# Selecting three batches early and running three experts while the last batch is selected

## What is computed

```python
logits = jnp.einsum('bsd,de->bse', x, Wg) + bg
probs = jax.nn.softmax(logits, axis=-2)          # over the tokens of a batch
vals, idx = jax.lax.top_k(jnp.transpose(probs, (0, 2, 1)), 128)
tok = x[bidx, idx]                               # 128 tokens per batch and expert
h = relu(einsum('bekd,edo->beko', tok, w1) + b1)
h = relu(einsum('bekd,edo->beko', h, w2) + b2)
h = einsum('bekd,edo->beko', h, w3) + b3
out = zeros.at[bidx, idx].add(h * vals)
```

## Time and profile before

| | us |
|---|---|
| median of 3 runs | 4139.88 (4139.71 to 4147.63) |
| profiled execution, its time | 4138.08 |
| its span, first to last instruction | 4136.3 |
| PE busy in the span | 3837.9 (93%) |
| DVE, ACT, POOL busy | 2483.1, 1566.9, 904.0 |
| granted clock, mean | 0.978 of full |

### The profile page before, as it was taken

How to read it: one execution, slowest core, us unless ns; L and a number is a source line. 1 busy time by engine, 2 the same in 40 slices (tenths; PEclk the granted TensorE clock), 3 DMA queues, 4 the chain that set the end, 5 groups by cost and what they waited for, 6 DMA issues and landing times. The chain is left out here.

```text
span 4136.3 us, 91192 instructions
## 1 busy us (share of the span) xinstructions
PE 3837.9 (93%) x36924; PEld 2346.8 (57%) x36924; DVE 2483.1 (60%) x4839; ACT 1566.9 (38%) x3178; POOL 904.0 (22%) x1017
## 2 busy tenths in 40 slices
PE   5999999999999999999999999999999948999996
PEld 2677645656776456567754565677545623444445
DVE  3777535877775368777744587777446872222224
ACT  2444225854442258544422584444135720000002
POOL 2333200223331012233310022333101202222221
PEclk8999999999999999999999999999999979999998
DMA  8333449744333487443335873433358725666676
GB/s 259 105 92 97 126 169 316 269 130 112 96 95 116 188 310 266 127 116 95 95 104 203 305 265 119 116 96 96 103 221 297 265 86 127 157 147 157 148 181 189
DMA packets 323147, 678.60 MB, mean 164 GB/s; under 512 B 28432, under 2 KB 125760, under 8 KB 319504
## 3 DMA queue, kind: packets, MB, share of 16 engines
q1 hardware_dynamic: 275152, 621.65, 46.9%
q0 software_dynamic: 15024, 34.41, 4.5%
q10 hardware_dynamic: 32576, 16.92, 1.9%
HBM read 388.31 MB, written 210.11 MB: 145 GB/s over the span
## 5 line engine op out<-in xcount | busy, mean ns | idle before, releaser
L530 ACT ACTIVATE sc<-sc,nmax 128x1024 f32<-128x1024 f32 x516 | 591.7, 1147 | 777.0 <-DVE nmax L756 776.4
L487 POOL TENSOR_SCALAR sc<-sc,pinv 128x1024 f32<-128x1024 f32 x516 | 576.5, 1118 | 1198.8 <-DVE pinv L764 1185.6
L1088 PE MATMUL psum<-pts,wct 32*64 32x256 f32 x8192 | 460.2, 376 | 9.0 <-PEq L1083 4.6
L1088 PE MATMUL psum<-xall,wct 32*64 32x256 f32 x8192 | 458.9, 376 | 6.1 <-issue 6.0
L1073 PE MATMUL psum<-xt,w_all 128*128 128x256 f32 x1792 | 415.7, 385 | 23.6 <-PEq L1070 23.6
L886 DVE CUSTOM_DVE_ANT_0 sc<-psum,big 128x896 f32<-128x896 f32 (+7 forms) x512 | 364.0, 753 | 102.9 <-PE psum L1294 87.2
L781 DVE STREAM_TRANSPOSE pts<-sc 128x1024 f32<-128x1024 f32 (+3 forms) x342 | 333.6, 976 | 130.6 <-PE psum L1088 87.0
L1073 PEld LDWEIGHTS psum<-xt,w_all 128*128 128x128 f32 x1792 | 332.5, 190 | 128.3 <-issue 67.0
L530 ACT ACTIVATE sc<-sc,xmax 128x896 f32<-128x896 f32 (+7 forms) x512 | 394.8, 773 | 11.7 <-DVE xmax L886 11.6
L756 DVE CUSTOM_DVE_ANT_0 sc<-psum,table_a 128x1024 f32<-128x1024 f32 x258 | 312.1, 1210 | 110.0 <-PE psum L1031 92.5
L1088 PEld LDWEIGHTS psum<-pts,wct 32*64 32x64 f32 x8192 | 310.6, 132 | 99.8 <-issue 54.8
(11 more groups left out here) (194 smaller groups left out, 5362.0 us busy)
## 6 DMA issues: line engine op xcount, KB each, us to landing
wct<-xall SPq DMA_DIRECT2D x576, 128.0 KB, 2.4
big<-skew_d SPq DMA_DIRECT2D x48, 1024.0 KB, 5.4
w_sb<-w_dram SPq DMA_DIRECT2D x45, 1024.0 KB, 5.7
big<-skew_d SPq DMA_DIRECT2D x48, 768.0 KB, 4.4
big<-skew_d SPq DMA_DIRECT2D x32, 896.0 KB, 5.3
big<-skew_d SPq DMA_DIRECT2D x32, 640.0 KB, 7.0
w_all<-wqkv_dram SPq DMA_DIRECT2D x33, 512.0 KB, 3.5
skew_d<-pts SPq DMA_DIRECT2D x8, 2048.0 KB, 6.6
```

The lines of the kernel that those rows point to most:

```text
L487: pool.tensor_scalar(sc[k % 4][:, :], sc[k % 4][:, :], pinv[:, k % 4:k % 4 + 1], 1.0, ALU.mult, ALU.mult).then_inc(probs_scaled, 1)
L530: act.activation(tile, tile, ACT.Exp, bias=least, scale=-1.0, accum_out=total).then_inc(probs_ready, 1)
L1088: mm = pe.matmul(OSUM[HEAD[h], a, :], v_all[rows, ST * (b % GROUPS) + b // GROUPS, HEAD[h]], ptf[h][rows, QG * b:QG * b + QG], start=(b == ...
```

## The change

Batches 0 to 2 stay in block 1's loop, batch 3 is written out behind it (`batch(B - 1, last=True)`). In the written-out batch:

- The selection of batches 0 to 2 (96 rows) runs on DVE inside self-attention. SP loads their logits during pair 0 (`load_held`), the maximum and the scaling stand at the first pair border, rounds 0 to 6 at the ends of pairs 1 to 7, rounds 7 to 15 between the row tiles of the output projection. PE turns and flips the lists there, DVE merges behind the first copied block, and PE waits for `picks_done` before the first relative product. The scratch tiles are parts of `xr` and `pts`, so `x` of batch 3 is loaded in two halves, the second after round 8.
- POOL gathers expert 0's tokens of batches 0 to 2 at unit 24 of cross-attention. SP loads expert 0's `w1` and `w2` at unit 26, in the place of the next batch's `xT`, weights and tables.
- The prefetch for a next batch is left out. PE transposes expert 0's tokens, then the normalized rows, then come the logits. SP copies them straight from SBUF to SBUF with eight DMAs.

In block 2, six steps stand ahead of the loop: experts 0, 1, 2 over batches 0 to 2, then the same experts over batch 3. Batch 3's selection (32 rows) runs on DVE under the first of them; ACT takes its exponentials behind step 0's second layer, PE turns its lists inside step 2's first layer. Tokens of these steps are transposed by PE and copied by ACT. Ahead of the loop, which now runs experts 3 to 13, the tokens of expert 3 and of expert 15 are gathered, turned and spread, the spreads on SP's queue ahead of the loop's loads.

```diff
+FIRST_EXPERTS = (0, 1, 2)
+F = len(FIRST_EXPERTS)
 LAST_EXPERTS = (E - 2, E - 1)
+SOONER, LATER = (0, 1, 2), (3,)
 FINISH = ((0, 1), (2,), (3,))
-STEPS = [(e, group) for group in FINISH for e in LAST_EXPERTS]
+STEPS = [(e, group) for group in (SOONER, LATER) for e in FIRST_EXPERTS] + \
+        [(e, group) for group in FINISH for e in LAST_EXPERTS]
 TAKEN = [sum(len(group) for _, group in STEPS[:s]) for s in range(len(STEPS) + 1)]
+BEHIND = 2 * F
+PICKS = TOPK // 8
+SOONER_ROWS, LATER_ROWS = E * len(SOONER), E * len(LATER)
 EXTRA = 2
 WXN = 3 * DC * P + EXTRA
...
+        def selection(dve, done, i, groups, pr, held, row_no, lists, above, best):
+
+            count, (lo, hi) = E * len(groups), (groups[0], groups[-1] + 1)
...
+            def scale_rows():
+
+                dve.wait_ge(row_exp_ready, 2 * i + 2)
+                done(dve.tensor_tensor(rinv[0:n, :], rsum[0:n, 0:1], rsum[0:n, 1:2], ALU.add))
+                done(dve.reciprocal(rinv[0:n, :], rinv[0:n, :]))
+                done(dve.tensor_scalar(held[0][0:n, :], held[0][0:n, :], rinv[0:n, 0:1], None, ALU.mult))
+
+            def pick(r):
+
+                now = held[r][0:n, :]
+                eight = top[0:n, 8 * r:8 * r + 8]
+                done(dve.max(eight, now))
+                ins = dve.max_index(top_at[0:n, 8 * r:8 * r + 8], eight, now)
+                if r < PICKS - 1:
+                    ins = dve.match_replace(held[r + 1][0:n, :], eight, now, -1.0)
+                done(ins)
+
+            def number_rows():
+
...
+                def load_held():
+
+                    sp.wait_ge(x2_stored, 32)
+                    sp.sem_inc(x2_stored, -32)
+                    sp.wait_ge(logits_stored, 16 * GROUPS)
+                    sp.dma_start(held_flip, flip_in).then_inc(flip_loaded, 16)
+                    flat = logit_d.rearrange("b e n -> (b e) n")
+                    for i in range(2):
+                        for j in range(2):
+                            sp.dma_start(held_pr[SOONER_ROWS * i:SOONER_ROWS * i + SOONER_ROWS, j, :],
+                                         flat[0:SOONER_ROWS, HALF * (i ^ j):HALF * (i ^ j) + HALF]
+                                         ).then_inc(held_loaded, 16)
 
                 def next_wqk(hp):
...
+                    sp.wait_ge(held_moved, 1)
+                    sp.dma_start(xr[:, ST // 2:ST, :], x[b, HALF:S, :].rearrange("(t p) d -> p t d", p=P)
+                                 ).then_inc(xr_loaded, 16)
...
+                        if u == PRELOAD[0]:
+                            for free in (w_free, *table_free):
+                                sp.wait_ge(free, 1)
+                            for n, w in enumerate((w1, w2)):
+                                sp.dma_start(w_front[n], w[0].rearrange("(c p) n -> p c n", p=P)).then_inc(we_loaded[n], 16)
+                        continue
...
+                                sp.dma_start(last_pr[E * i:E * i + E, j, QG * k:QG * k + QG],
+                                             last_lg[DH * g:DH * g + E, :]).then_inc(lg_loaded, 16)
+                    return
...
+                    if last and u == NU // 2:
+                        pool.wait_ge(picks_done, 1)
+                        pool.wait_ge(xt_free, 1)
+                        for b in SOONER:
+                            pool.indirect_dma_start(tok[:, b, :], None, x2_d[0:S * len(SOONER), :],
+                                                    bass.IndirectOffsetOnAxis(ap=rows[:, b, 0:1], axis=0)
+                                                    ).then_inc(step_gathered[b], 16)
...
+                    copy_first_tokens(act, 0, tokT)
+                    root_of_variance()
+                    even_transposes(x2t)
+                    return
...
+                    dve.memset(top[:, :], 0.0)
+                    dve.wait_ge(held_loaded, 64)
+                    row_max()
+                    cross_border(scale_rows)
                     add_biases()
+                    pick(0)
+                    for hp in range(2, PAIRS):
+                        cross_border()
+                        add_biases()
+                        pick(hp - 1)
...
+                    if last and t < 5:
+                        for r in range((7, 9, 11, 13, 14)[t], (9, 11, 13, 14, 16)[t]):
+                            pick(r)
+                        if t == 0:
+                            dve.sem_inc(held_moved, 1)
+                        if t == 4:
+                            number_rows()
+                    if last and t == ST - 2:
+                        copy_lists((BANK[6][:, 0:P], BANK[7][:, 0:P]))
...
+                    odd_transposes(x2t)
+                    dve.wait_ge(logits_ready, 1)
+                    done(dve.tensor_scalar(last_lg, LOGITS, bg_sb[:, 0:1], None, ALU.add))
+                    dve.sem_inc(logits_out, 1)
+                    return
...
+                    if last and t == ST - 1:
+                        turn_picks(pe, 0, held_row_no, (BANK[6][:, 0:P], BANK[7][:, 0:P]))
...
+                    first_tokens(pe, 0)
+                    transpose_rows()
...
+            sp.dma_start(w_e[2], w3[0].rearrange("(c p) n -> p c n", p=P)).then_inc(we_loaded[2], 16)
+            sp.dma_start(flip[:, :], flip_in).then_inc(flip_loaded, 16)
+            for j in range(F - 1):
+                for n, w in enumerate((w1, w2, w3)):
+                    sp.dma_start(first_w[j + 1][n], w[FIRST_EXPERTS[j + 1]].rearrange("(c p) n -> p c n", p=P)
+                                 ).then_inc(next_w_loaded[j], 16)
             sp.wait_ge(x2_stored, 32)
-            sp.dma_start(flip[:, :], flip_in).then_inc(flip_loaded, 16)
-            for n in range(2):
-                sp.sem_inc(we_free[n], 1)
-            with sp.Fori(0, E - 2) as e:
+            for n, w in enumerate((w1, w2, w3)):
+                sp.dma_start(last_w[n][:, :, :], w[E - 1].rearrange("(c p) n -> p c n", p=P)
+                             ).then_inc(last_w_loaded, 16)
+            def spread(dst, src, loaded):
+
+                for g in range(GROUPS):
+                    for m in range(GROUPS):
+                        sp.dma_start(dst[DH * m:DH * m + DH, :, g, :, :], src[DH * g:DH * g + DH, :, m, :, :]
+                                     ).then_inc(loaded, 16)
+
+            sp.wait_ge(early_turned, B)
+            sp.sem_inc(tok_free, 1)
+            sp.wait_ge(tokT_free, 1)
+            sp.sem_inc(tokT_free, -1)
+            spread(tokT, tok_blocks, tokT_loaded)
+            sp.wait_ge(early_turned, 2 * B)
+            sp.sem_inc(tok_free, 1)
+            spread(last_tokT, last_blocks, last_tokT_loaded)
+            with sp.Fori(F, E - 2) as e:
                 for n, w in enumerate((w1, w2, w3)):
...
+            gather_sooner(1)
+            for s in range(F):
+                for i in range(2):
+                    scatter(s, i)
+                if s + 2 < F:
+                    gather_sooner(s + 2)
+                scatter(s, 2)
+                if s + 2 == F:
+                    gather_later()
+            pool.wait_ge(first_turned, DC * (F + 1))
+            gather(F)
+            gather_last()
+            for s in range(F, BEHIND):
+                scatter(s, 0)
+            for b in range(B):
+                pool.wait_ge(scattered[b], 16 * F)
...
+            for s in range(F):
+                bend(s, 0)
+                bend(s, 1)
+                if s == 0:
+                    row_exps(act, 1, last_pr[0:2 * LATER_ROWS, :, :])
+                    act.wait_ge(bias3_scaled, 1)
+                take_y(s, 0)
+                take_y(s, 1)
+                copy_first_tokens(act, s + 1, tokT if s < F - 1 else later_tokT)
+                take_y(s, 2)
+            act.wait_ge(bias3_scaled, 2)
+            for s in range(F, BEHIND):
+                bend(s, 0)
+                bend(s, 1)
+                take_y(s)
+            with act.Fori(F, E - 2):
...
+            turn_tokens(tok_blocks, gathered, 16, early_turned)
+            turn_tokens(last_blocks, [last_gathered] * B, 16 * B, early_turned)
+            with dve.Fori(F, E - 2) as e:
...
-                        if s == 0 and layer == 1 and c == 1:
-                            dve.wait_ge(blocks_free, 1)
-                            turn_tokens(E - 1)
...
+                if s < F:
+                    w, tokens = first_w[s], tokT
+                    if s == 0:
+                        pe.wait_ge(we_loaded[0], 16)
+                        pe.sem_inc(we_loaded[0], -16)
+                    else:
+                        pe.wait_ge(next_w_loaded[s - 1], 48)
+                    pe.wait_ge(tok_copied, DC * (s + 1))
+                elif s < BEHIND:
+                    w, tokens, slots = first_w[e], later_tokT, slice(e, e + 1)
...
+                    if s == F - 1 and o == 0:
+                        turn_picks(pe, 1, row_no[:, :], (BANK[0][:, 0:P], BANK[0][:, P:2 * P]))
+                    if s == F - 1 and o == 1:
```

(11 more changed lines are left out.)

512 lines of the change are left out of this document (304 added, 208 removed).

## The result

The changed kernel takes 4078.7 us (median of four runs, 4075.4 to 4081.0) where the kernel before takes 4143.8 beside it (four runs, 4139.7 to 4148.0): a ratio of 0.984, with a 95% interval of 0.983 to 0.986. The forecast was 4071, with a range of 4057 to 4090. The two profiled executions differ by 59.9 us (4138.08 to 4078.16), where the sum had said 67.0; the medians differ by 65.0, because the kernel before had a median of 4139.88 when the forecast was made and of 4143.8 here, so the profiles are the fairer test of the sum. Granted clock over the whole span: 0.978 before, 0.983 after.

What follows compares the result with a forecast made beforehand. PE, busy 93% of the span, was taken as the bound, so only its idle stretches or removed work give time. Terms -76.1 + 3.1 + 6.7 + 10.5 - 11.8 + 0.6 = -67.0 from 4138.08 gave 4071 us, range 4057 to 4090.

Steps and rivals of the forecast that it cites:

- forecast case: Whole kernel: the summed working comes true, 4064 to 4078 us, chance 0.63.
- part 7: Batch 3: inserted selection rounds and early gathers almost hidden, costing PE 0.6 us.
- Part 1: Tail of batch 3: without prefetch and selection hole, expert 0 starts at 3357.8 instead of 3433.9, 76.1 us gained.
- Part 2: Expert 0's start: PE's clock is low after 5 us of idling, 3.1 us lost.
- Part 3: Six small steps before the loop: 130.3 us for what costs 123.6, 6.7 us lost.
- Part 4: Batch 3's selection under the first steps: just covered, cost 0, margin 0.3 us.
- Part 5: Loop's head: first weights queue behind two spreads, 7.4 us wait plus 3.1 for clock, 10.5 us lost.
- Part 6: Behind the expert loop: waits for hid and last_tokT and their clock loss go, 11.8 us gained.
- Not hidden: Rival, batch 3: inserted rounds delay PE, up to 2.65 us seven times plus 3, 4075 to 4092; chance 0.12.
- picks late: Rival, small steps: batch 3's picks come 5 to 20 us late, 4075 to 4090; chance 0.12.
- no overlap: Rival, step 0: some wait puts it behind the whole selection, only the tail's 26 us gained, 4120; chance 0.03.
- clock stays at half: Rival, six small steps: PE's clock stays at half, 130 us more, 4198, slower than before; chance 0.02.

Runs made afterwards that it cites:

- f8: Changed kernel with each of the sixteen selection rounds of batches 0 to 2 done twice: 4094.6 us.
- e1: Changed kernel with SP loading expert 3's w1 and w2 ahead of the two token spreads, and w3 behind them: 4070.4 us.
- f7: Changed kernel with four of the sixteen rounds of batch 3's selection done twice: 4085.4 us.
- g1: Changed kernel with the edits of e1, f5 and f6, and PE's wait before the loop for step 5's take moved to ACT: 4054.9 us.
- f5: Kernel of e1 with GpSimd scattering step 3's result before gathering expert 15's tokens: 4067.2 us.
- e2: Kernel of e1 with expert 15's tokens gathered, turned and spread behind the loop again: 4076.7 us.
- g3: Changed kernel unaltered, measured again on the same chip and in the same rounds as g1 and g2: 4076.1 us.
- f6: Changed kernel with SP issuing the eight transfers of batch 3's logits at the head of the second block: 4071.9 us.
- e3: Changed kernel with unused filler products for PE in batch 3's tail, eight before the normalized rows and one behind rows 1 to 6: 4077.4 us.
- g2: Kernel of g1 with shorter filler products for PE than in e3, five before the rows and one behind odd rows but the last: 4056.0 us.

## Why the prediction was right, and where it was off

The measured 4078.7 lies in the range, but 0.7 us above the band of the forecast case itself (4064 to 4078); the range reaches further for rivals that did not come. Of the 7.1 us by which the sum is off, the start of expert 0 has +7.4 (+6.8 with the 0.6 of part 7), the six steps -1.7, the loop's head +2.5 and the end -0.5.

*Part 1, the tail.* The mechanism holds; expert 0 starts 7.4 us later than worked out. Of this 3.2 lie ahead of the tail: the normalization ends at 3347.4 instead of 3344.2, because batches 1 and 2 took 825.2 and 824.0 us instead of 822.05 and 822.65 (the first store of x2 was 0.65 late as well, and the last batch 2.05 shorter). Over all kernels run here these two lie at 820.6 to 825.2, and the last one at 819.0 to 826.1 (f8's doubled rounds aside): scatter between executions, which a sum over one execution can't foresee. The other 4.2 were mis-sized: the rows' pace is 1.96 us and not 1.6 (last copy 1.4 late), the logits 3.35 and not 1.92 (1.4), the eight transfers 4.97 and not 3.72 (1.25), the border 0.2 more (its 0.6 had no row), and the hand-over from logits to SP 0.3 less. The first two are the clock: the working kept the kernel before's durations for PE, although it took out the very work that fills PE beside them. The third is a term priced by a row of another form, a store to DRAM. How the 4.2 are shared out differs between executions of the same instructions: the rows' pace was 1.50 us in e1, f7 and g1, the logits took 1.92 in f5, and there the transfers took 6.43. The sum of them was too small every time: expert 0 starts 15.9 to 17.6 us behind x2's store in the changed kernel, e1, e2, f5, f7 and g3, where the working had 12.9.

*Part 2, the clock.* 3.1 was said, 1.7 measured (12.16 for 10.48), and 1.5 to 2.4 behind the same wait in e1, e2, f5, f7 and g3; in f6, with a wait of 1.24 us, it was 0.1. The nearest row of before priced it too high. That row isn't 32 products at a clock of 0.50 either, as the prediction reads it: the earlier trace rows covers 3 us, and products of 7.07 us that take 10.14 have run at half for some 6 us (an estimate, twice the 3.07).

*Part 3, the steps.* 131.7 less 1.7 is 130.0, against 130.3. The agreement hides two errors: steps 0 to 2 take 97.2 without the clock's share, not 98.4 (twelve transposes add 1.31, not 1.64), and steps 3 to 5 take 32.85, not 31.9. A 384-column layer takes 10.48 at a pace of 10.32, midway between its neighbours as interpolated.

*Part 4, batch 3's selection.* Covered, as said. The margin is 4 us, not 0.3, since DVE's rounds come 2.37 us apart (38.6 us with the scaling, from the exponentials' sum at 3391.13 to the numbering at 3429.72) where the working took 2.65 from the rounds of before. The diff had the reason, and the working passed over it: the new `pick` no longer waits between `max_index` and `match_replace`, one wait of three in a round, and the trace shows the one's load of values at 3424.74, before the other ends at 3424.81:

```profile
3424.14 0.67 DVE L365 FIND_INDEX8 top_at<-top,left 32x8 uint32<-32x512 f32 x1
3424.74 0.06 DVE L367 MATCH_VALUE_LOAD left<-top,left 32x8 f32 x1
3424.80 0.66 DVE L367 MATCH_REPLACE8 left<-top,left 32x512 f32<-32x512 f32 x1
3425.61 0.68 DVE L364 MAX8 top<-left 32x8 f32<-32x512 f32 x1
```

ACT's switch of function shows

```profile
3388.28 1.28 ACT L340 ACT_TABLE_LOAD   x1
3389.58 0.72 ACT L340 ACTIVATE w_and_tables<-w_and_tables,rmax 32x512 f32<-32x512 f32 x1
```

and so again 1.30 us from load to exponential. The Trainium skill (ScalarE: Activation LUTs, What ACT_TABLE_LOAD costs) counts 2.66 with a drain; no drain is seen here, and the wait of 1.1 us that it would have made is absent. With the true margin even 2.66 would have been covered.

*Part 5, the loop's first weights.* The forecast's wait came, where it was said and for the reason that was said (e1), and it was 10.97 us instead of 7.4. Scatter, copy, gathers and turns were right to 0.2 us: SP begins its spreads 12.5 us behind the last product's end at 3464.04, 12.3 in the sum. Then the second spread began 1.0 late and took 11.2 instead of 10.6, w1 was issued at 35.9 instead of 33.6, and PE began 7.9 us behind that issue where the median landing is 5.7; the landing itself took 7.5, and the bound of 10.5 had covered this. PE itself came 0.95 later than said, which takes as much off. With the same code at this place PE began 7.3 (g3), 6.5 (e3), 6.3 (f6) and 6.3 us (f7) behind the issue and waited 9.64, 7.85, 8.10 and 8.05 us, so the profiled execution is the longest of five and the forecast's 7.4 lies just below them all. Why the landing scatters wasn't tried; each time the load was issued right behind 16 other transfers. The Trainium skill's fit (DMA: Bandwidth & Descriptors, Anatomy of one DMA) gives an estimate of 4.4 us, and the page makes it for transfers that GpSimd issues. The loads here are SP's, and the trace lies further from that estimate than from the 5.7. What the working didn't see is the second half of the early turn's price: expert 15's gathers also stood ahead of step 3's scatter on GpSimd, which was for the most part hidden by SP's wait and came out in e1. In the changed kernel it is the 0.52 us of wait in step 5; with the scatter moved, steps 3 to 5 take 32.4 us (f5) and 32.1 (g1).

*Part 6, the end of the loop.* -11.8 forecast, -12.3 in the profile and 11.8 in e2 against e1, where other waits make up the same sum.

*Part 7, the inserted work.* No cost can be seen, as said: the last batch took 820.0 us, but it scatters from 819.0 to 826.1, so one of 3 us wouldn't show. f8 shows room for a second round at each pair end, and for some 5 us in all in the output projection. "Not hidden" (4075 to 4092) is the rival whose times the result meets, but not its mechanism: what made 4078.7 of 4071 is the tail and the loop's head. The rivals "picks late", "no overlap" and "clock stays at half" showed nothing; f7 shows how near the first was.

## What to carry to other kernels

When a wait is removed by overlapping, also ask what clock the engine keeps once its filler work is gone, and which transfers an engine has to issue before a border that all engines leave together: here those could go behind it at no cost. A step moved earlier is paid on every queue that it is moved past, and the dearer queue hides the others: take them away one after another and measure again. Margins that come out near zero are worth a run that spends a known amount of them.

## What was not expected of the hardware

- Indirect gathers take longer beside plain loads: with two loads of 1 MB in flight, the last of four gathered tiles is turned 6.8 (e1), 8.3 (f5) and 7.7 us (g1) behind its gather's issue; without them 3.9.
- SP issues transfers between SBUF tiles at 0.62 us each (4.97 for 8), where stores to DRAM took 0.465. The same eight, in the same place, took 4.99 (e1), 5.36 (e2), 5.70 (e3), 5.81 (g3) and 6.43 us (f5); what makes the difference is open.
- The clock behind a wait: 11.9 to 13.3 us for expert 0's first layer behind 6.6 to 8.1 us of idle time, 10.56 behind 1.24 (f6) and 1.23 (g2), but 12.16 behind 1.22 in g1. The wait alone doesn't settle it; what tells g1 from f6 is open.
